# An mLSTM decoder layer on Trainium2: the router's product and its first routing step stand in the first unit of the next iteration, not in the third unit ahead of the norm's sums

## What is computed

```python
x = x + attention(layernorm(x))                      # causal, 16 heads of 16
x = x + mlstm(layernorm(x), ctx, ctx)                # 8 heads of 32, gated decays
x = x + moe(layernorm(x))                            # 8 experts of 1024, top 2

# mlstm, for each batch and head
log_d = lf[t] - lf[s] + i_pre[s]      (s <= t),  m = max_s log_d
s_mat = (q @ k.T / sqrt(32)) * exp(log_d - m)
h     = s_mat @ v / (max(|sum_s s_mat|, exp(-m)) + 5e-5)
h     = h * rsqrt(mean(h*h) + 1e-6) * gain

# the router of the mixture
logits = layernorm(x) @ router_w + router_b          # 256 x 8
probs  = softmax(logits); the two largest are the token's weights
```

## Time and profile before

| | us |
|---|---|
| median of 3 runs | 990.98 |
| lowest and highest run | 987.38, 990.99 |
| span of the profiled execution | 996.1 |

### The profile page before, as it was taken

One profiled execution on the slowest core, in us unless ns is written; L12 is line 12 of the kernel. 1 busy time (PEld: TensorE's weight loads), 2 busy tenths in 40 slices (PEclk: granted clock), 3 DMA queues, 4 the chain that ended last, 5 costly groups with the idle time before them and its releaser, 6 DMA issues.

```text
span 996.1 us, 31655 instructions
## 1 busy us (share of the span) xinstructions
PE 890.7 (89%) x11877; PEld 661.9 (66%) x11966; DVE 606.8 (61%) x1340; ACT 486.2 (49%) x810; POOL 526.7 (53%) x660
## 2 busy tenths in 40 slices
PE   4799999999997687899989888899999999999995
PEld 3566666667665354656656576687787878787783
DVE  4767778677675445776767667455555555555552
ACT  3567677677666356455555544233333333333331
POOL 2556657557555334387777767543444434353442
PEclk9999999999997789788888999999999999999998
DMA  9112443443435643444445323332323323232221
GB/s 288 52 45 54 112 114 81 108 114 80 117 104 117 161 154 101 130 150 146 162 149 166 116 65 88 83 76 49 50 46 54 50 44 53 47 51 49 50 34 22
DMA packets 133198, 92.97 MB, mean 93 GB/s; under 512 B 75712, under 2 KB 114112, under 8 KB 132928
## 3 DMA queue, kind: packets, MB, share of 16 engines
q1 hardware_dynamic: 119760, 73.10, 26.3%
q0 software_dynamic: 13296, 17.83, 10.3%
HBM read 54.65 MB, written 37.32 MB: 92 GB/s over the span
## 4 chain that ended last, share of the span: by engine, by line
PE 62%; DVE 10%; DMA 6%; ACT 6%; issue 5%; POOL 4%; SPq 3%; another core or an unknown queue 1%; DVEq 0%; POOLq 0%; ACTq 0%
PE pair L951 18%; PE pair L965 9%; PE pair L967 7%; PE pair L644 4%; PE pair L666 3%; PE pair L680 3%; PE pair L822 3%; DMA o_scr<-On 2%; DMA STG<-wup_in 2%; POOL sm L1571 2%; PE pair L617 2%; DVE SD L1147 2%; PE pair L693 2%; ACT PT L1348 2%; PE pair L836 2%
## 5 line engine op out<-in xcount | busy, mean ns | idle before, releaser
L951 PE MATMUL pair<-XTs,WU 128*128 128x128 bf16 x3408 | 285.5, 220 | 12.8 <-issue 6.0
L951 PEld LDWEIGHTS pair<-XTs,WU 128*128 x3408 | 238.6, 98 | 82.3 <-issue 19.3
L1608 POOL DMA_INDIRECT out_d<-XB x71 | 115.4, 1625 | 212.6 <-DVE XB L1313 189.0
L1484 ACT ACTIVATE Hf<-pair 128x512 f32<-128x512 f32 x142 | 84.8, 598 | 222.6 <-PE pair L951 210.7
L965 PE MATMUL pair<-WD,Hh 128*128 x479 | 181.6, 380 | 0.0
L1304 DVE CAST Hh<-Hf 128x512 bf16<-128x512 f32 x142 | 64.5, 454 | 172.4 <-ACT Hf L1484 158.9
L967 PE MATMUL pair<-WD,Hl 128*128 x568 | 155.0, 273 | 5.3 <-issue 0.5
L1529 POOL TENSOR_SCALAR_AFFINE_SELECT PT<-PT 128x512 f32<-128x512 f32 (+1 forms) x96 | 74.7, 792 | 56.5 <-ACT PT L1342 51.1
L1306 DVE TENSOR_TENSOR Hl<-Hf,Hh 128x512 bf16<-128x512 f32 x142 | 99.8, 703 | 4.9
L1037 DVE TENSOR_REDUCE mxn<-pair 128x4 f32<-128x1024 f32 x64 | 75.3, 1218 | 26.7 <-PE pair L625 26.6
L1147 DVE TENSOR_TENSOR SD<-pair,SD 128x1024 f32<-128x1024 f32 x48 | 58.7, 1223 | 51.5 <-ACT SD L1426 28.7
(11 more groups left out here) (241 smaller groups left out, 1804.3 us busy)
## 6 DMA issues: line engine op xcount, KB each, us to landing
XB<-xs_scr SPq DMA_DIRECT2D x71, 130.0 KB
STG<-wup_in SPq DMA_DIRECT2D x32, 256.0 KB, 4.5
q_scr<-SPL SPq DMA_DIRECT2D x16, 512.0 KB, 4.2
STG<-wdn_in SPq DMA_DIRECT2D x32, 256.0 KB, 2.7
o_scr<-On SPq DMA_DIRECT2D x32, 128.0 KB, 4.1
Mm<-o_scr SPq DMA_DIRECT2D x16, 256.0 KB, 2.8
CnT<-ctxt_in SPq DMA_DIRECT2D x16, 256.0 KB, 4.2
CX<-ctx_in SPq DMA_DIRECT2D x16, 256.0 KB
```

The lines of the kernel that those rows point to most:

```text
L951: t = e.matmul(upb(j, k)[:, 128 * (fm % 4):128 * (fm % 4) + 128], WU[:, bass.ds(reg[j] * 4096 + off, 128)], XTs[:, r, hx, dk, :], start=n ...
L1484: e.activation(Hf[:, r, hs], upb(j, k), ACT.Gelu).then_inc(gel.sem, 1)
L1608: e.indirect_dma_start(out=out, out_offset=bass.IndirectOffsetOnAxis(ap=XS[:, i % NX, 256:257].bitcast(I32), axis=0), in_=Yf[:, i % NY, :] ...
```

## The change

B6 and R1 move from unit 2 of an iteration to unit 0 of the next one. In unit 2, B6 stood ahead of B4 and R1 was the last step; in unit 0 they stand behind B4x (and R6), R1 now in odd iterations, 5 to 15. In the tail B6 of batch 12 is written out. The waits of B6 for the shared bank are now counted from the list, and name the last B4, R1 and R5 ahead of it.

```diff
@@ mlstm_steps, u == 0
                 if ok(i - 5) and i % 2 == 0:
                     yield "R6", i - 5, 0
                     ready += 8
+                if ok(i - 4):
+                    yield "B6", i - 4, 0
+                if ok(i - 4) and i % 2:
+                    yield "R1", i - 4, 0
@@ u == 2
-                if ok(i - 3):
-                    yield "B6", i - 3, 0
                 if ok(i - 4) and i % 2:
                     yield "R4", i - 4, 0
                 if ok(i - 1):
@@
                     yield "R5", i - 4, 0
-                if ok(i - 3) and i % 2 == 0:
-                    yield "R1", i - 3, 0
@@ tail
-    tail = (("PV", z, 1), ("B4x", a), ...
+    tail = (("PV", z, 1), ("B6", z - 3), ("B4x", a), ...
@@
+        def last_before(kind, at, b):
+
+            done = [s[1] for s in bsteps[:next(i for i, s in enumerate(bsteps) if s[:2] == (at, b))] if s[0] == kind]
+            return done[-1] if done else -1
@@ tensor_mlstm, B6
-                    w.wait_ge(ms_.sem, ms_.at(min(b + 1, B - 1)))
-                    w.wait_ge(rd1.sem, rd1.at(odd_to(b - 1)))
-                    w.wait_ge(rd5.sem, rd5.at(odd_to(b - 2)))
+                    w.wait_ge(ms_.sem, ms_.at(last_before("B4", "B6", b)))
+                    w.wait_ge(rd1.sem, rd1.at(last_before("R1", "B6", b)))
+                    w.wait_ge(rd5.sem, rd5.at(last_before("R5", "B6", b)))
```

More of the change, by code:

```diff
@@ L218, in mlstm_steps @@
     a = B - 2
-    tail = (("PV", z, 1), ("B4x", a), ("R6", z - 4), ("experts", 1), ("PV", z, 2), ("B3", z), ("B4o", a), ("B5s", a), ("B5", z - 2), ("experts", 4),
+    tail = (("PV", z, 1), ("B6", z - 3), ("B4x", a), ("R6", z - 4), ("experts", 1), ("PV", z, 2), ("B3", z), ("B4o", a), ("B5s", a), ("B5", z - 2), ("experts", 4),
             ("B6", z - 2), ("B5n", a), ("experts", 2), ("B4", z), ("B4p", z), ("experts", 4), ("R1", z - 2), ("experts", 6),
```

## The result

The changed kernel takes 1014.51 us in the median of 4 runs (1013.14 to 1014.82), the kernel before 989.58 (4 runs beside them): a ratio of 1.0268, 95% interval 1.0237 to 1.0298. It is slower by 24.9 us; the prediction said slower, by 9.5, and its range ended at 1010.

A forecast was written before the change was run, and what follows sets the result against it. PE was busy 89% of 996.1 us; even halves were tied to POOL and PE, odd ones to DVE and PE. (15.4 - 13.5) x 5 = +9.5 on the median 990.98 gave 1000.5; range 988 to 1010.

The forecast's parts named there:

- The two holds: Odd power-to-power window (half), T its start: POOL's remainder holds R1, then R2 or R3 by 0.9 us; half 15.4.
- rival 2: Odd halves: R1's DVE operations pass unheld; half 13.6, +0.5 us, 991.5, no change; chance 0.2.
- Rivals 1, 2 and 3: Odd halves: 1, first hold only, 996, chance 0.15; 3, PE and clock set them, 984.5, 0.12; 2 is rival 2.
- I take the held case at full clock: Odd halves: both holds, with no slower PE clock counted; half 15.4, +9.5 us over five.
- the upper bound: PE's sums and the rest at the slower clock in odd halves: about 1.2 us each, +6 over five.
- The idle of PE ahead of D of unit 2: PE in odd iterations: its idle there grows to over 1 us.
- The even halves stay: Even power-to-power windows: unchanged, 13.6 to 14.2 us.
- Iterations 4 and 5 "at zero": Iteration 5: B6 leaving unit 2 of iteration 4 brings the power 1 us forward, R1 takes 1.3 back; counted zero.
- B6 "costs and gives nothing": B6's eight matmuls, 1.06 us, leave unit 2 and return in unit 0; zero net, but R4 loses cover.
- rival 4: PE, unit 0: B6's wait for `ms_` costs nothing unless DVE's B4 chain is held, then about 0.5 us, hidden; no separate chance.

The follow-up runs named there:

- PE kept at work: Changed kernel with 14 and 18 matmuls that nobody reads, given to PE in odd iterations; ratio to the kernel before 1.0110.
- R1 behind the multiplication: Changed kernel with R1 one step later on every engine, after unit 1's multiplication instead of ahead of it; ratio to the kernel before 1.0139.
- remainder first with B6 back: Changed kernel with POOL's unit 0 remainder ahead of the scatters in odd iterations from 7, and batch 0's B6 in unit 2 of iteration 3; ratio 1.0050.
- R1 alone: Changed kernel with B6 put back in unit 2, so that only R1 is moved to unit 0; ratio to the kernel before 1.0206.
- after again: Changed kernel run and profiled a second time without edit; ratio to the kernel before 1.0182, stage from first to last power 233.6 us.
- before again: Kernel before, profiled once more without edit; one run, 1000.19 us, stage from first to last power 215.4 us.
- the remainder first: Changed kernel with POOL's unit 0 remainder right behind the power, ahead of the scatters, in odd iterations from 7 on; ratio to the kernel before 1.0062.
- no remainders in either kernel: POOL's remainder replaced by a memset in both kernels, low parts of 32 weight chunks left out; ratios 1.0011 (changed kernel) and 1.0095 (kernel before).

## Why the prediction was right in its direction and too small

**The two holds: right.** For R1 I had L1201's like held until T + 6.67, R1 done at T + 7.1, the multiplication at T + 7.05, the remainder at T + 10.85, a second hold of 0.9, and `mb_` at T + 12.4. (From the variance at T + 9.45 and the 1.3 us behind it the remainder's place is T + 10.75; the 10.85 in the text is a slip.) The trace has T + 6.71, 7.16, 7.19, 10.97, 0.92 (1.11 instead of 0.19) and 12.47. That a DVE operation which starts ahead of the remainder is held all the same, as in the earlier trace rows, is again the case: L1201 began 0.52 us ahead of it. By the lock of the Trainium skill (SBUF — State Buffer, "SBUF: two separate sides"), where the first to start wins, L1201 would have passed and rival 2 have come true; by the recorded starts the trace disagrees. Starts on POOL are rough in a profile, so whether the remainder really began later isn't shown. Rivals 1, 2 and 3 fell.

**The step that failed: "I take the held case at full clock".** My odd half was 15.4, with nothing for the clock; it is 15.37 in the run in which PE is kept at work, 15.34 in iteration 7 of the changed kernel's second profile, and 16.60 in the first. The time from `mb_` to the next power has two values, one for each level of the clock: 16.60 - 12.47 = 4.13 in the changed kernel, 4.12 with R1 behind the multiplication, but 15.37 - 12.49 = 2.88 and 13.65 - 10.76 = 2.89 where the sums take 0.59 (2.4 GHz) and not 0.99 (1.2 GHz). So the clock costs 1.25 per odd half. I had that number, 1.2 x 5 = +6, as the upper bound. With 1.25 in each, the five halves would come to +15.7; they measure +15.4 in the first profile. Four of them are the forecast and the clock; the fifth, 16.52, is so long partly by luck: a third hold (L997, 0.93 us) brings `mb_` to T + 13.23, and only 3.29 follow. The idle of PE ahead of D of unit 2, which I forecast at over 1 us, was there (1.73, waiting for ACT's `SD`); I drew a bound from it and no term of the sum.

**"The even halves stay": wrong, by 1.8 us in one and by 0.4 each in the others.** Iteration 14 grew by 1.84. The shifted order brought a remainder beside a conversion on DVE:

```profile
562.04 1.86 DVE L1262 CAST TEie<-TEe 128x16 int32<-128x16 f32 x1
```

The changed kernel's second profile has the same, 1.90 us and a half of 15.75. In eleven other profiles the conversion took 0.17 or 0.18, and where R1 was moved and it was so short, iteration 14 took 14.02 to 14.13 at mean clocks of 0.88 to 1.00. So this growth goes with the hold, though the clock was lower with it, 0.82 and 0.83.

The other four even ones grew by 0.2 to 0.7, 0.4 on average, and they have the hold of L1180 ahead of the power. Before, B4's chain was held in iterations 10 and 12 only (L1174 1.55 us, L1175 1.79). Where it is not held, iterations 8, 10 and 12 are 13.43 to 13.46 at a mean clock of 1.00 (PE kept at work; remainder first with B6 back), and with R1 alone iterations 10 and 12 are 13.60 and 13.57 at 0.88, iteration 8 with the hold 14.00. So this is a hold as well, and not the clock alone. I had read such a hold, the 1.55 us of L1174, and did not ask where the change would put it.

**Iterations 4 and 5 "at zero", and B6 "costs and gives nothing": wrong.** B6's new wait for `ms_`, my rival 4, stops PE in iteration 4:

```profile
395.75 1.51 PE L881 MATMUL pair<-WR,x3T 128*128 128x8 f32 x8 [2.06 <-DVE sm L1181]
```

I had read the margin of 0.3 us in iteration 11 and used it for all; and it is 2.06 us with nothing of B4 held, where rival 4 had 0.5 and a hold. The wait is worth about 0.5 us of the half: 11.68 with it and 11.18 without, at clocks of 0.82 and 0.83. But the kernel before, run again, took 12.10 there at 0.81, and 11.33 at 0.97 in its first profile; at like clock the change does not lengthen iteration 4, and the +1.3 goes with the clock, 0.97 against 0.73. Whether PE's wait is what lowered the clock isn't shown. Iteration 5 is the other way round. At a clock of about 0.7 it took 17.22 before and 18.21 after; at 0.8, 15.98 before, 16.97 with R1 in unit 0 and 17.30 with R1 behind the multiplication. That is the 1.0 to 1.3 of R1 that I had reckoned there; the 1 us that B6's leaving was to give back did not come. In odd iterations B6's new place gains where the clock is low, 0.6 in iteration 11: behind a late R1 it would stand in R4's way.

**The reference.** 9.5 + 5.9 (what the odd halves measure beyond it, mostly clock) + 1.8 + 1.3 + 1.0 + 1.7 = 21.2 us is the stage in the profiles. The medians say 24.9; the 3.7 between lie outside the stage or in the spread of executions.

This split is that of one pair of profiles. In the second pair (after again, before again) the stage is 18.2 us longer, and the odd halves 7 to 15 carry only 10.6 of it, as two and not four of them have the slow sums; iterations 5, 6 and 14 carry 2.2, 3.4 (a half of 17.23 at a mean clock of 0.66) and 1.7. What repeats is the holds and the two values behind `mb_`. Which halves get the lower clock doesn't.

**Is it all the holds?** On ratios: the change costs 1.8% beside the later runs (2.7% in the first); with the remainder first 0.5 to 0.6% stays. With no remainders in either kernel the change costs nothing. Shown is that the holds, and the lower clock that follows them, carry about two thirds of the cost by the first comparison and all of it by the second, in which the kernel before lost 0.95% itself. What the last 0.5% is stays open. Iteration 15 is a candidate that no run took away: it is still held with the remainder first, 17.44 and 15.73 us, where before took 13.34 and 13.69; but the stage as a whole was then 214.7 in one profile, as short as before's 215.4, and 222.8 in the other. Open is too what makes the clock stay low through a whole half (17.2 to 17.6 us) in one execution and not in the next.

## What to carry to other kernels

A step of small VectorE operations that is moved must be laid against every GpSimd operation that has held one before (here the remainder), in its new place, and then once more behind the delay that the first meeting makes: here the first hold of 1.6 us pushed the chain into a second, and in four of five iterations moving one GpSimd operation undid both. The steps that did not move must be laid against it too: the shifted order put new holds into the even halves. A forecast stall on the path should carry the lower clock with it as a term with a chance of its own, and not as the bound alone, when the profile of before has both levels for the same matmuls. And a margin read in one iteration is not that of the first and the last ones.

## What the runs showed of the hardware

By the recorded starts, which are rough on POOL, the hold begins before the remainder does: by 0.52 us (L1201) and by 0.66 (the conversion, at 562.04 with the remainder at 562.70). Both times a scatter stands right ahead of the remainder on POOL's queue. The scatter alone did not do it: L1199 at 507.44, inside the one of 507.19 to 508.16, took 0.19 us, and so did L1201 at 501.07 inside one in the changed kernel without remainders. Nor did a remainder with no scatter right ahead: L1220 at 506.09, with R1 behind the multiplication, began 0.06 us ahead of the remainder of 506.15 and took 0.19.

Operations with one input can be held too: the conversion 1.86 us, and L1000 1.32. A reduction in the middle of a remainder was not (L1198 in the run with R1 behind the multiplication, 0.19 us at 501.33, the remainder 501.16 to 502.33), nor was an operation with a PSUM operand (L1194 with B6 back, 0.69 us at 493.86, the remainder from 493.81).

The power, 2.9 us long with two SBUF inputs, did not hold L1194 inside it. The memset held no operation with two inputs (L1217 at 506.15, 0.17 us, the memset 506.06 to 506.58), but an operation with one input that began beside one lasted until it ended; DVE and POOL in the changed kernel without remainders:

```profile
561.73 0.60 DVE L997 TENSOR_SCALAR LS<-LS 128x2 f32<-128x2 f32 x1
...
561.76 0.54 POOL L1572 MEMSET WD<- 128x512 bf16 x1
```

Giving PE 32 unread matmuls in each odd iteration brought the mean granted clock of iteration 11 from 0.68 to 1.00. The even halves 8, 10 and 12, which got none of them, became 0.7 to 0.8 us shorter and lost their hold; the two are not told apart there.
